# Reordering the grouped-query cross attention of a four-layer model on one Trainium2 core: its first units, the split product, the small turns, and GpSimd's loads

## The chip, the cores and the metric

The program is one launch on one NeuronCore of a Trainium2 chip. The metric is device time in microseconds, the median of several runs. Before the change it is 1155.62 us (three runs, 1152.46 to 1157.61). The engines named below are TensorE (PE for its matmuls, PEld for its weight loads), VectorE (DVE), ScalarE (ACT), GpSimd (POOL) and SyncE (SP), which issues most DMAs. Each runs its own list of instructions in order, and they wait for one another by semaphores.

## The reference, cut to what matters

The model runs twelve blocks on `x` of 2 x 128 tokens with 256 features. The change is in the tenth, `_L3_xattn_ref`, in which the 128 queries of each batch attend to 2048 context rows and to the tokens themselves:

```python
q = (x @ wq).reshape(B, L, 16, 128)
k = (x @ wk).reshape(B, L, 4, 128)
v = (x @ wv).reshape(B, L, 4, 128)
q = rms_norm(q, q_norm_w)
k = rms_norm(k, k_norm_w)
k_ctx = rms_norm((h_ctx_kv @ wk_ctx).reshape(B, T, 4, 128), k_norm_w)
v_ctx = (h_ctx_kv @ wv_ctx).reshape(B, T, 4, 128)
q = q * cos + rotate_half(q) * sin
k = k * cos + rotate_half(k) * sin
k_full = jnp.repeat(jnp.concatenate([k_ctx, k], axis=1), 4, axis=2)
v_full = jnp.repeat(jnp.concatenate([v_ctx, v], axis=1), 4, axis=2)
scores = jnp.einsum('blhd,bmhd->bhlm', q, k_full) * scale + mask
probs = jax.nn.softmax(scores, axis=-1)
out = jnp.einsum('bhlm,bmhd->blhd', probs, v_full)
return out.reshape(B, L, 2048) @ wo
```

All of it is in float32. T is 2048, and `mask` is causal on the tokens' own 128 keys. The last block of the model, a gated feed-forward layer in rounded numbers, has weights that are prepared while this attention runs.

## The kernel before, in words

The class `Wide` holds this block. Its work is cut in two ways. A **unit** `u` (0 to 31) is one head of one batch: 16 chunks of 128 context keys and one chunk of own keys. A **group** `g` (0 to 31) is one quarter (512 rows) of the context of one key head of one batch: its keys are made by `key`, its values by `value`, each with 16 weight loads and 16 matmuls in the trace (one `pe.matmul` of float32 operands shows as two of each). Five groups of keys are made ahead (`FRONT = 5`), so that unit `u` makes group `g = u + 5` beside its own attention.

The **front** (`front_tensor`, and the first lines of `scalar`, `vector` and `gpsimd`) projects the six pieces of batch 0 (keys, four times four query heads, values), rotates them on VectorE (`rope`), scales them on ScalarE (`scale_heads`), turns them on TensorE (`turn_heads`) and copies them back (`copy_turned`). For the keys of groups 0 to 4, ScalarE squares them (`square`), VectorE sums (`sum_squares`), GpSimd takes the inverse root (`scales`), VectorE multiplies (`normalize`), TensorE turns them (`turn_keys`) and ScalarE copies them to their place (`copy_keys`, which raises the semaphore `w_kt`).

The **loop** over the units is in `tensor`. TensorE does, in this order: `scores` of `u` (32 loads and 3 more); `turn_last_output` of `u - 2`; `product` of `u - 1` in three parts (chunks 0 to 8, 9 to 11, 12 to 16, that is 18, 6 and 10 loads), with `turn_largest` of `u` behind the first and `spread_largest` of `u` behind the second; and then `between_tensor`: `turn_keys` of group `g - 1`, `value` of `g`, a wait for `w_kt`, in the first six units one piece of batch 1's projection, in five of them a `turn_heads`, and `key` of `g`.

VectorE's chain in a unit is: largest score of each half (`largest_of`), with `normalize` of group `g - 1` between the two; the larger of both; after `turn_largest` the largest over the partitions; a diagonal matrix of it; after `spread_largest` the copy of the spread row; two additions that shift the scores (`shift`), for which the exponentials of ScalarE and the next unit's `scores` wait. Behind them stand the division of unit `u - 1`, in units 1, 2, 4, 5 and 6 a `rope` of batch 1, and `sum_squares` of group `g`.

From unit 18 on, each unit also prepares one of twelve pieces of the last block's weights: VectorE takes the exponent and a multiple (`weights_exponent`, `weights_multiple`), and GpSimd adds and subtracts (`weights_gpsimd`) and issues the load of the piece after next (`weights_load`), all before its `scales` of the group.

Below, T of a unit is the start of the weight load of its `turn_largest` (L2206 before), Z that of its `spread_largest` (L2211), and S that of its `scores` (L2180).

Of the kernel before, what the change touches and what calls it, by code (L numbers as in the profile page):

```python
# [1892 lines left out]
class Wide:  # L1893
# [180 lines left out]
    def value(self, pe, g, bank):  # L2074
# [7 lines left out]
        for t in range(4):  # L2082
# [3 lines left out]
        last.then_inc(k.s("w_v"), 1)  # L2086
# [55 lines left out]
    def front_tensor(self, pe):  # L2142
# [17 lines left out]
        self.turn_keys(pe, 0, 3)  # L2160
        self.key(pe, 4, 6)
# [29 lines left out]
    def turn_last_output(self, pe, u):  # L2191
# [74 lines left out]
    def tensor(self, pe):  # L2266
        k, s = self.k, self.k.s
        self.front_tensor(pe)
        for u in range(self.UNITS + 1):
            if u < self.UNITS:  # L2270
                self.scores(pe, u)
            if u >= 2:
                self.turn_last_output(pe, u)
            if u >= 1:
                self.product(pe, u - 1, range(0, 9))
# [6 lines left out]
            if u >= 1:  # L2282
                self.product(pe, u - 1, range(12, MC + 1))
# [779 lines left out]
```

## Time and profile before

| what | value |
|---|---|
| median of 3 runs | 1155.62 us (1152.46 to 1157.61) |
| the profiled execution's own time | 1157.82 us |
| its span | 1155.9 us |
| TensorE matmul busy | 1049.1 us (91%) |
| VectorE busy | 700.8 us (61%) |
| ScalarE busy | 503.6 us (44%) |
| GpSimd busy | 232.1 us (20%) |
| front and units of this block | 630.57 to 1086 us of the span |

The durations below come from the profiled execution. Its time is 2.2 us above the median, and its span lies 1.9 us below its time. In a timeline row of the trace the first number is the start in microseconds, the second how long the group of instructions took, then come engine, line, operation and operands, the count, and in brackets the idle time ahead of it with what ended it.

### The profile page before, as it was taken

To read this page: it belongs to the slowest core of one execution; us is meant where nothing else is said; L and a number is where in the kernel's file an instruction comes from. 1 tells how busy PE (TensorE), PEld (TensorE's weight loads), DVE (VectorE), ACT (ScalarE), POOL (GpSimd) and SP (SyncE) were. 2 spreads that over 40 slices of the span, in tenths; PEclk is the share of its full clock that TensorE was granted. 3 is DMA by queue.
4 is the path that set the end of the run, shared out by engine and by line. 5 is a ranking of instruction groups with operands and counts; after the bars stand their busy time and mean duration, and the time that the engine had idled before them with its cause. 6 is when DMAs were issued, how large, how long until landed. Compare 5 with 4: busy or idle time off the path is not lost.

```text
span 1155.9 us, 23193 instructions
## 1 busy us (share of the span) xinstructions
PE 1049.1 (91%) x9488; PEld 847.5 (73%) x9488; DVE 700.8 (61%) x1337; ACT 503.6 (44%) x867; POOL 232.1 (20%) x356
## 2 busy tenths in 40 slices
PE   6899999989999879999987889989999999999885
PEld 3655678865666645677765668889999999999763
DVE  3646242347777358888643766765665566667466
ACT  3042221125666338888754523333233232232374
POOL 4501038402132000000010411210100133332030
PEclk9998999997999979999999989999999999999898
DMA  9711246554663517000141200131111112100000
GB/s 381 292 72 62 87 153 230 182 140 115 181 180 100 170 39 249 3 2 2 38 147 37 92 25 31 37 110 41 53 37 38 55 58 79 57 19 10 1 2 10
DMA packets 39188, 104.57 MB, mean 90 GB/s; under 512 B 4144, under 2 KB 12720, under 8 KB 37424
## 3 DMA queue, kind: packets, MB, share of 16 engines
q1 hardware_dynamic: 35184, 91.55, 24.2%
q0 software_dynamic: 2752, 9.44, 2.4%
q10 hardware_dynamic: 1152, 2.16, 0.5%
q8 instruction: 73, 1.20, 0.4%
q14 instruction: 27, 0.22, 0.1%
HBM read 87.93 MB, written 15.20 MB: 89 GB/s over the span
## 4 chain that ended last, share of the span: by engine, by line
PE 72%; DVE 13%; ACT 4%; issue 4%; POOL 4%; DMA 2%; DVEq 0%; SPq 0%; POOLq 0%; ACTq 0%
PE ps L2225 9%; PE ps L433 7%; PE ps L2180 7%; PE ps L1413 5%; PE ps L1764 5%; PE ps L426 4%; PE ps L2070 4%; PE ps L488 3%; PE ps L1755 3%; PE ps L1561 3%; PE ps L2084 2%; PE ps L1091 2%; PE ps L1099 2%; PE ps L1572 2%; DVE st L1690 2%
## 5 line engine op out<-in xcount | busy, mean ns | idle before, releaser
L2225 PE MATMUL ps<-vv,prob 128*128 128x129 f32 x1024 | 128.7, 274 | 0.0
L2225 PEld LDWEIGHTS ps<-vv,prob 128*128 128x128 f32 x1024 | 122.5, 192 | 0.0
L1690 DVE TENSOR_REDUCE st<-ps 128x1 f32<-128x512 f32 x128 | 83.5, 687 | 27.3 <-PE ps L1561 21.1
L2348 DVE TENSOR_REDUCE probT<-ps 128x128 f32<-128x1024 f32 x64 | 82.6, 1290 | 28.4 <-PE ps L2180 20.4
L2115 ACT ACTIVATE kt<-ps,w 128x512 f32<-128x512 f32 x32 | 22.1, 689 | 141.8 <-PE ps L2092 141.8
L433 PE MATMUL ps<-xT,big 128*128 128x256 f32 x352 | 79.8, 381 | 1.4 <-ACT xT L715 0.7
L2360 DVE TENSOR_TENSOR prob<-ps,probT 128x1024 f32<-128x1024 f32 x64 | 79.6, 1286 | 1.1
L2321 ACT ACTIVATE prob<-prob 128x1024 f32<-128x1024 f32 x64 | 70.8, 1107 | 19.6 <-DVE prob L2360 19.5
L1637 ACT ACTIVATE prob<-ps 128x1024 f32<-128x1024 f32 x64 | 65.8, 1030 | 28.7 <-PE ps L1572 27.0
L152 POOL TENSOR_SCALAR small<-small 128x4 f32<-128x4 f32 (+1 forms) x44 | 12.0, 273 | 325.7 <-DVE small L2122 175.3
L433 PEld LDWEIGHTS ps<-xT,big 128*128 128x128 f32 x352 | 66.4, 190 | 11.8 <-DVE prob L504 1.9
L2070 PE MATMUL ps<-qz,big 128*128 128x128 f32 x512 | 63.0, 277 | 5.0 <-ACT w L1992 2.4
L2070 PEld LDWEIGHTS ps<-qz,big 128*128 128x128 f32 x512 | 59.7, 192 | 9.9 <-ACT w L1992 4.5
L2084 PE MATMUL ps<-qz,big 128*128 128x128 f32 x512 | 62.3, 275 | 0.0
L2180 PE MATMUL ps<-w,kt 128*128 128x128 f32 x512 | 59.9, 275 | 0.8 <-ACT kt L2115 0.8
L2180 PE MATMUL ps<-big,kt 128*128 128x128 f32 x512 | 59.9, 275 | 0.8 <-ACT kt L2115 0.8
L2084 PEld LDWEIGHTS ps<-qz,big 128*128 128x128 f32 x512 | 59.8, 192 | 0.2
L2180 PEld LDWEIGHTS ps<-big,kt 128*128 128x128 f32 x512 | 58.8, 192 | 1.2 <-ACT kt L2115 1.0
L2180 PEld LDWEIGHTS ps<-w,kt 128*128 128x128 f32 x512 | 58.5, 192 | 1.1 <-ACT kt L2115 1.1
L2122 DVE TENSOR_REDUCE small<-probT 128x4 f32<-128x512 f32 x30 | 20.6, 685 | 62.8 <-ACT probT L2105 62.8
L504 DVE TENSOR_TENSOR prob<-prob,ps 128x512 f32<-128x512 f32 x22 | 15.1, 688 | 67.9 <-ACT prob L497 67.8
L2294 ACT COPY w<-ps 128x128 f32<-128x128 f32 x32 | 8.5, 266 | 109.3 <-PE ps L2189 109.3
(456 smaller groups left out, 2216.1 us busy)
## 6 DMA issues: line engine op xcount, KB each, us to landing
big<-ctxT_in SPq DMA_DIRECT2D x36, 512.0 KB, 4.1
big<-blocks_in SPq DMA_DIRECT2D x22, 768.0 KB, 4.4
key_parts<-w POOLq DMA_DIRECT2D x16, 384.0 KB, 5.0
kt<-key_parts SPq DMA_DIRECT2D x32, 192.0 KB, 3.3
vv<-ctx_in SPq DMA_DIRECT2D x2, 2176.0 KB, 27.3
vv<-early_values SPq DMA_DIRECT2D x4, 1088.0 KB, 12.1
kt<-ctxT_in SPq DMA_DIRECT2D x2, 2048.0 KB, 13.2
kt<-key_parts SPq DMA_DIRECT2D x32, 128.0 KB, 3.2
```

Source lines behind the costliest of these rows:

```text
L433: last = pe.matmul(out, w[:, c, lo:lo + P], xT[:, :, c, :], start=(c == 0), stop=(c == DC - 1))
L1413: last = pe.matmul(self.k.ps[g:g + 17, bank, 0:P], self.values(u, ch), pT[:, ch * P:(ch + 1) * P], start=(ch < 4), stop=(ch + 4 >= MC))
L1637: act.activation(self.pT[:, u % 2, h * 1024:(h + 1) * 1024], k.bank(2 + 2 * h, 1024, 2), ACT.Exp).then_inc(s("exp"), 1)
L1690: dve.tensor_reduce(self.mx[:, u % 2, n:n + 1], k.ps[:, n % 2, :], AX.X, ALU.max).then_inc(s("reduced"), 1)
L1764: last = pe.transpose(k.ps[:, bank, ch * P:(ch + 1) * P], self.p[u % 4][:, (4 * n + ch) * P:(4 * n + ch + 1) * P], k.const("ident"))
L2070: last = pe.matmul(k.ps[:, bank, t * P:(t + 1) * P], self.stage[:, g % 2, c, t * P:(t + 1) * P], self.ctx("wk_ctx", DC)[:, c, h * DH:(h + ...
L2084: last = pe.matmul(k.ps[:, bank, t * P:(t + 1) * P], self.stage[:, slot, c, t * P:(t + 1) * P], self.ctx("wv_ctx", DC)[:, c, h * DH:(h + 1 ...
L2180: last = pe.matmul(k.ps[:, ch // 4, ch % 4 * P:ch % 4 * P + P], keys[:, ch * P:(ch + 1) * P], q, start=True, stop=True)
L2225: last = pe.matmul(k.ps[:, 7, 0:DH + 1], self.prob(u)[:, ch * P:ch * P + P], v, start=(ch == 0), stop=(ch == MC))
L2321: act.activation(e, e, ACT.Exp).then_inc(s("c3_exp"), 1)
L2348: dve.tensor_reduce(self.largest[:, h * P:(h + 1) * P], bank.rearrange("p (c t) -> p t c", t=P), AX.X, ALU.max).then_inc(s("c3_max"), 1)
L2360: dve.tensor_tensor(self.prob(u)[:, lo:hi].rearrange("p (c t) -> p c t", t=P), k.bank(0, hi, 5)[:, lo:hi].rearrange("p (c t) -> p c t", t= ...
```

## The change

No arithmetic is added or removed. The instructions of four engines are written in another order.

- In the loop, `turn_last_output` moves behind the first part of `product`, so that it stands beside `turn_largest`; `product` has two parts (chunks 0 to 8, and 9 to 16), and `spread_largest` stands behind the second.
- In `between_tensor` the wait for `w_kt` stands ahead of `value`, in all units. In units 1 and 4 `value` is cut in two halves around the projection; in units 2, 3, 5, 6 and 7 `turn_heads` comes before it; in units 6 and 7 `key` comes before `value`.
- Unit 0 does both small turns behind the projection, and group 4 is normalized in the front.
- In the front, `key` of group 4 takes bank 3 and comes ahead of the turned keys; ScalarE, VectorE and GpSimd follow in a new order.
- GpSimd issues the load of a weight piece behind `scales` of its unit, no longer ahead of it.

```diff
-    def value(self, pe, g, bank):
+    def value(self, pe, g, bank, tiles=range(4)):
...
@@ between_tensor
-        if g not in self.FIRST_VALUES:
-            self.value(pe, g, 5)
+        if u in self.TURN_AT:
+            self.turn_heads(pe, 1, self.TURN_AT[u], 5)
+        elif u in (1, 4):
+            self.value(pe, g, 5, range(0, 2))
         pe.wait_ge(s("w_kt"), g)
         if u < 6:
             self.project(pe, 1, u, 6)
+        if u == 0:
+            self.turn_largest(pe, u)
+            self.spread_largest(pe, u)
+        if u in (6, 7):
+            self.key(pe, g, 6)
         if u in self.TURN_AT:
-            pe.wait_ge(s("w_v_sb"), g + 1)
-            self.turn_heads(pe, 1, self.TURN_AT[u], 5)
+            pe.wait_ge(s("w_q"), 5 + self.TURN_AT[u] + 1)
+        if u >= 1:
+            self.value(pe, g, 5, range(2, 4) if u in (1, 4) else range(4))
         if u < 6:
             pe.wait_ge(s("w_heads"), 6 + u + 1)
-        self.key(pe, g, 6)
+        if u not in (6, 7):
+            self.key(pe, g, 6)
@@ tensor
-            if u >= 2:
-                self.turn_last_output(pe, u)
             if u >= 1:
                 self.product(pe, u - 1, range(0, 9))
-            if u < self.UNITS:
+            if u >= 2:
+                self.turn_last_output(pe, u)
+            if 1 <= u < self.UNITS:
                 self.turn_largest(pe, u)
             if u >= 1:
-                self.product(pe, u - 1, range(9, 12))
-            if u < self.UNITS:
+                self.product(pe, u - 1, range(9, MC + 1))
+            if 1 <= u < self.UNITS:
                 self.spread_largest(pe, u)
-            if u >= 1:
-                self.product(pe, u - 1, range(12, MC + 1))
             self.between_tensor(pe, u)
@@ front_tensor
         self.turn_heads(pe, 0, 2, 2)
-        self.turn_keys(pe, 0, 3)
-        self.key(pe, 4, 6)
+        self.key(pe, 4, 3)
+        self.turn_keys(pe, 0, 6)
         self.turn_keys(pe, 1, 7)
...
@@ scores
+            if u == 0 and ch == 12:
+                pe.wait_ge(s("w_kn"), self.FRONT)
@@ scalar, in the loop
+            if self.TURN_AT.get(u, 0):
+                self.scale_heads(act, 1, self.TURN_AT[u])
             if u >= 2:
                 self.copy_output(act, u - 2, P)
             if g - 1 < self.GROUPS:
                 self.copy_keys(act, g - 1, 6)
...
@@ gpsimd, from unit 18 on
             if u >= self.EIGHT_AT:
                 eight.weights_gpsimd(pool, o, dram, u - self.EIGHT_AT)
             self.scales(pool, o, g)
+            if u >= self.EIGHT_AT:
+                eight.weights_load(pool, dram, u - self.EIGHT_AT + 2)
```

TensorE, a middle unit of the loop from chunk 8 of `product` on, before. L2225 is `product`, L2206 and L2211 the two small turns, L2092 `turn_keys`, L2084 `value`, L2070 `key`, L2180 `scores`.

```order
L2225 MATMUL ps<-vv,prob 128x129 [waits c3_exp]
L2206 MATMUL ps<-const,probT 128x128 [waits c3_max]
L2225 MATMUL ps<-vv,prob 128x129 x3
L2211 MATMUL ps<-probT,const 128x128 [waits c3_max]
L2225 MATMUL ps<-vv,prob 128x129 x4
L2225 MATMUL ps<-probT,prob 128x129
L2092 MATMUL ps<-const,big 128x128 [waits w_kn]
L2092 MATMUL ps<-const,big 128x128 x3
L2084 MATMUL ps<-qz,big 128x128 [waits w_stage0,c3_aT]
L2084 MATMUL ps<-qz,big 128x128 x7
L2070 MATMUL ps<-qz,big 128x128 [waits w_stage0,w_kt]
```

The same unit now (`product` is L2226, the turns L2207 and L2212, `turn_keys` L2093, the turned output L2192).

```order
L2226 MATMUL ps<-vv,prob 128x129 [waits c3_exp]
L2192 MATMUL ps<-const,xn 128x128 [waits c3_finished,w_v_sb]
L2207 MATMUL ps<-const,probT 128x128 [waits c3_max]
L2226 MATMUL ps<-vv,prob 128x129 x7
L2226 MATMUL ps<-probT,prob 128x129
L2212 MATMUL ps<-probT,const 128x128 [waits c3_max]
L2093 MATMUL ps<-const,big 128x128 [waits w_kn]
L2093 MATMUL ps<-const,big 128x128 x3
L2084 MATMUL ps<-qz,big 128x128 [waits w_stage0,w_kt,c3_aT]
L2084 MATMUL ps<-qz,big 128x128 x7
L2070 MATMUL ps<-qz,big 128x128 [waits w_stage0]
```

The spread has moved from between two parts of `product` to its end, and the wait for `w_kt` from the first matmul of `key` to the first of `value`, right behind `turn_keys`.

TensorE, the end of unit 0's scores up to unit 1's, before and now (L426 is the projection).

```order
-L2206 MATMUL ps<-const,probT 128x128 [waits c3_max]
-L2211 MATMUL ps<-probT,const 128x128 [waits c3_max]
-L2092 MATMUL ps<-const,big 128x128 [waits w_kn]
-L2092 MATMUL ps<-const,big 128x128 x3
+L2093 MATMUL ps<-const,big 128x128 [waits w_kn]
+L2093 MATMUL ps<-const,big 128x128 x3
 L426 MATMUL ps<-big,xT 128x512 [waits w_kt]
 L426 MATMUL ps<-big,xT 128x512
+L2207 MATMUL ps<-const,probT 128x128 [waits c3_max]
+L2212 MATMUL ps<-probT,const 128x128 [waits c3_max]
 L2070 MATMUL ps<-qz,big 128x128 [waits w_stage1,w_heads]
```

The two small turns have moved behind the turned keys and the projection, which used to wait for them.

GpSimd in one of the units from 18 on, before: the sum and the difference of a weight piece (L2631, L2632), the load of a piece (L2624) and `scales` (L152, L153).

```order
L2631 TENSOR_TENSOR w<-w,qwrow 128x512 [waits e8_power]
L2632 TENSOR_TENSOR big<-w,qwrow 128x512 [waits pool_order]
L2624 DMA w<-w_in 128x512 [waits e8_w]
L152 TENSOR_SCALAR small<-small 128x4 [waits w_kn,w_ssq]
L153 TENSOR_TENSOR small<-small,const 128x4 [waits pool_order]
```

Now:

```order
L2650 TENSOR_TENSOR w<-w,qwrow 128x512 [waits e8_power]
L2651 TENSOR_TENSOR big<-w,qwrow 128x512 [waits pool_order]
L152 TENSOR_SCALAR small<-small 128x4 [waits w_kn,w_ssq]
L153 TENSOR_TENSOR small<-small,const 128x4 [waits pool_order]
L2643 DMA w<-w_in 128x512 [waits e8_w]
```

The DMA has moved from ahead of `scales` to behind it.

## Rows read from the trace of the kernel before

**Rows 1.** The page's chain that ended last, shares by engine.

```profile
PE 72%; DVE 13%; ACT 4%; issue 4%; POOL 4%; DMA 2%; DVEq 0%; SPq 0%; POOLq 0%; ACTq 0%
```

**Rows 2.** Windows: stretch, length, then busy time (count) by engine, clock, DMA, GB/s.

```profile
800.00:850.00 50.00, 49.87 (x442) 49.05 (x441) 32.10 (x50) 16.59 (x24) 4.81 (x8) 1.00 0.14 43
```

**Rows 3.** Timeline of TensorE's weight loads, unit 9, from T on.

```profile
800.65 0.14 PEld L2206 LDWEIGHTS ps<-const,probT 128*128 128x128 f32 x1
800.76 0.75 PEld L2225 LDWEIGHTS ps<-vv,prob 128*128 128x128 f32 x6
801.73 0.30 PEld L2211 LDWEIGHTS ps<-probT,const 128*128 128x128 f32 x2 [0.23 <-DVE probT L2356]
...
803.51 1.86 PEld L2084 LDWEIGHTS ps<-qz,big 128*128 128x128 f32 x16
```

**Rows 4.** Timeline, VectorE behind the spread of unit 10 (its Z is 814.14).

```profile
814.67 0.29 DVE L2358 COPY probT<-ps 128x128 f32<-128x128 f32 x1 [0.58 <-PE ps L2211]
815.00 2.49 DVE L2360 TENSOR_TENSOR prob<-ps,probT 128x1024 f32<-128x1024 f32 x2
```

**Rows 5.** Timeline, the spread's weight loads of units 1, 8, 18 and 27.

```profile
683.23 0.30 PEld L2211 LDWEIGHTS ps<-probT,const 128*128 128x128 f32 x2 [0.23 <-DVE probT L2356]
...
789.32 0.30 PEld L2211 LDWEIGHTS ps<-probT,const 128*128 128x128 f32 x2 [0.23 <-DVE probT L2356]
...
920.34 0.30 PEld L2211 LDWEIGHTS ps<-probT,const 128*128 128x128 f32 x2 [0.23 <-DVE probT L2356]
...
1037.27 0.30 PEld L2211 LDWEIGHTS ps<-probT,const 128*128 128x128 f32 x2 [0.23 <-DVE probT L2356]
```

**Rows 6.** Timeline, TensorE's loads around `turn_keys` of unit 27.

```profile
1038.61 0.47 PEld L2092 LDWEIGHTS ps<-const,big 128*128 128x128 f32 x4
...
1040.09 3.65 PEld L2180 LDWEIGHTS ps<-big,kt 128*128 128x128 f32 x32 [1.02 <-ACT kt L2115]
```

**Rows 7.** Timeline, units 24 and 25: GpSimd, then VectorE's `normalize`, then TensorE.

```profile
1005.90 0.60 POOL L2624 DMA_DIRECT2D w<-w_in  x1 [0.30 <-POOL big L2632]
...
1006.58 0.19 POOL L152 TENSOR_SCALAR small<-small 128x4 f32<-128x4 f32 x1
...
1007.91 0.69 DVE L2136 TENSOR_TENSOR big<-ps,small 128x512 f32<-128x512 f32 x1 [0.94 <-POOL small L153]
...
1010.25 0.14 PEld L2206 LDWEIGHTS ps<-const,probT 128*128 128x128 f32 x1 [0.54 <-DVE probT L2353]
```

**Rows 8.** Timeline of unit 1, from projection to the scales of its group.

```profile
686.90 1.88 PE L426 MATMUL ps<-big,xT 128*128 128x512 f32 x4
...
689.45 1.86 PEld L2070 LDWEIGHTS ps<-qz,big 128*128 128x128 f32 x16 [1.50 <-ACT qwrow L1992]
...
690.88 0.69 DVE L2017 TENSOR_TENSOR att<-att,small 128x512 f32<-128x512 f32 x1
...
692.17 0.69 DVE L2122 TENSOR_REDUCE small<-probT 128x4 f32<-128x512 f32 x1 [0.59 <-ACT probT L2105]
...
693.23 1.01 POOL L153 TENSOR_TENSOR small<-small,const 128x4 f32<-128x4 f32 x1
```

**Rows 9.** Timeline, end of the front: group 4's square, the first scores.

```profile
655.78 0.60 ACT L2105 ACTIVATE probT<-ps 128x512 f32<-128x512 f32 x1 [0.80 <-PE ps L2070]
...
660.63 3.65 PEld L2180 LDWEIGHTS ps<-w,kt 128*128 128x128 f32 x32 [1.07 <-ACT kt L2115]
```

**Rows 10.** Windows, unit 0.

```profile
667.00:674.00 7.00, 5.43 (x10) 2.42 (x10) 3.25 (x5) 3.10 (x4) 0.00 (x0) 0.51 0.00 0
```

**Rows 11.** Timeline, spread of unit 30 and scores of unit 31.

```profile
1067.40 0.30 PEld L2211 LDWEIGHTS ps<-probT,const 128*128 128x128 f32 x2 [0.22 <-DVE probT L2356]
...
1069.93 3.76 PEld L2180 LDWEIGHTS ps<-big,kt 128*128 128x128 f32 x32
```

**Rows 12.** The page's costliest groups: the exponentials.

```profile
L2321 ACT ACTIVATE prob<-prob 128x1024 f32<-128x1024 f32 x64 | 70.8, 1107 | 19.6 <-DVE prob L2360 19.5
```

**Rows 13.** Timeline, late `turn_heads` of unit 6.

```profile
765.43 0.42 PEld L2036 LDWEIGHTS ps<-const,attT 128*128 128x128 f32 x4 [1.78 <-issue]
```

More of the change, by code:

```diff
@@ L2081, in value @@
         pe.wait_ge(k.s(f"w_stage{slot}"), 16 * loads)
-        for t in range(4):
+        for t in tiles:
             for c in range(DC):
@@ L2085, in value @@
                                  self.ctx("wv_ctx", DC)[:, c, h * DH:(h + 1) * DH], start=(c == 0), stop=(c == 1))
-        last.then_inc(k.s("w_v"), 1)
+        if t == 3:
+            last.then_inc(k.s("w_v"), 1)
     def turn_keys(self, pe, g, bank):
@@ L2271, in tensor @@
                 self.scores(pe, u)
+            if u >= 1:
+                self.product(pe, u - 1, range(0, 9))
             if u >= 2:
                 self.turn_last_output(pe, u)
-            if u >= 1:
-                self.product(pe, u - 1, range(0, 9))
-            if u < self.UNITS:
+            if 1 <= u < self.UNITS:
                 self.turn_largest(pe, u)
             if u >= 1:
-                self.product(pe, u - 1, range(9, 12))
-            if u < self.UNITS:
+                self.product(pe, u - 1, range(9, MC + 1))
+            if 1 <= u < self.UNITS:
                 self.spread_largest(pe, u)
-            if u >= 1:
-                self.product(pe, u - 1, range(12, MC + 1))
             self.between_tensor(pe, u)
@@ L2299, in scalar @@
             self.copy_heads(act, 0, n, bank)
+        self.scale_heads(act, 0, 1)
         self.square(act, 0, 6)
@@ L2302, in scalar @@
         self.copy_turned(act, 0, 0, 0)
-        self.scale_heads(act, 0, 1)
-        self.square(act, 2, 4)
         self.copy_turned(act, 0, 1, 1)
         self.scale_heads(act, 0, 2)
+        self.square(act, 2, 4)
         self.square(act, 3, 5)
         self.copy_turned(act, 0, 2, 2)
-        self.copy_keys(act, 0, 3)
         self.scale_heads(act, 0, 3)
-        self.square(act, 4, 6)
+        self.square(act, 4, 3)
+        self.copy_keys(act, 0, 6)
         self.copy_keys(act, 1, 7)
@@ L2327, in scalar @@
                 self.copy_keys(act, g - 1, 6)
-            if self.TURN_AT.get(u, 0):
-                self.scale_heads(act, 1, self.TURN_AT[u])
+            if u in self.TURN_AT:
+                self.copy_turned(act, 1, self.TURN_AT[u], 5)
+            if u == 0:
+                self.copy_heads(act, 1, u, 6)
             if u < self.UNITS:
                 exp(u, 0)
-            if g < self.GROUPS and g not in self.FIRST_VALUES:
+            if u in (6, 7):
+                self.square(act, g, 6)
+            if 1 <= u < 6:
+                self.copy_heads(act, 1, u, 6)
+            if u >= 8 and g < self.GROUPS:
                 self.copy_value(act, g, 5)
@@ L2335, in scalar @@
                 exp(u, 1)
-            if g < self.GROUPS:
-                if u < 6:
-                    self.copy_heads(act, 1, u, 6)
-                if u in self.TURN_AT:
-                    self.copy_turned(act, 1, self.TURN_AT[u], 5)
+            if 1 <= u < 8:
+                self.copy_value(act, g, 5)
+            if g < self.GROUPS and u not in (6, 7):
                 self.square(act, g, 6)
@@ L2364, in vector @@
         k, s, F = self.k, self.k.s, self.FRONT
-        for n in range(3):
+        for n in range(4):
             self.rope(dve, o, 0, n)
@@ L2368, in vector @@
         self.sum_squares(dve, 1)
-        self.rope(dve, o, 0, 3)
+        self.rope(dve, o, 0, 4)
         for g in range(2):
@@ L2373, in vector @@
         self.sum_squares(dve, 3)
-        self.rope(dve, o, 0, 4)
         for g in range(2, 4):
@@ L2377, in vector @@
         self.sum_squares(dve, 4)
+        self.normalize(dve, 4, self.key_bank(4))
         for u in range(self.UNITS + 1):
@@ L2413, in gpsimd @@
         self.ones(pool, o)
-        for n in (1, 2):
+        for n in (1, 2, 3):
             self.query_scales(pool, o, 0, n)
@@ L2417, in gpsimd @@
             self.scales(pool, o, g)
-            if g % 2:
-                self.query_scales(pool, o, 0, 3 + g // 2)
+            if g == 1:
+                self.query_scales(pool, o, 0, 4)
         for g in range(4, self.GROUPS):
@@ L2619, in weights_load @@
         s = self.k.s
+        if i >= self.PIECES:
+            return
         if i < 2:
```

13 lines of the change are left out of this document (5 added, 8 removed).

## The prediction
> **What bounds the kernel now.** I read the chain of waits first: TensorE has 72% of it [rows 1]. Of windows over the attention, the one over units 9 to 13 shows TensorE busy 49.87 of 50 us at granted clock 1.00 [rows 2]. There the bound is how fast TensorE takes weight loads: 16 of them take 1.86 us, which is 15 spacings of 0.11 and the last one's 0.19 [rows 3]. From here on one load is 0.1116 us. What TensorE waits for must then be looked for in the timeline of weight loads, since the modelled ends of matmuls hide it. In a middle unit that timeline has one gap, ahead of the spread [rows 3]. Unit 8's spread starts at 789.32 and unit 9's at 801.73 [rows 5, 3]: a unit takes 12.41 us, which is 109 loads (12.16), less 0.05 for short ones, and a stall of 0.30. So the stage from unit 8 on is issue with one small stall, units 0 to 7 have larger ones [rows 8, 13], and in units 18 to 27 the spreads stand (1037.27 - 920.34)/9 = 12.99 us apart [rows 5], so something slower than TensorE's own work sets the pace.
>
> **The change, part by part.** I follow T (load of `turn_largest`), Z (load of the spread) and S (first load of scores).
>
> *The spread behind the product.* Six loads after T the spread would have been due at 800.76 + 6 x 0.1116 = 801.43, and it started at 801.73 [rows 3]: 0.30 lost in each unit. With 16 loads between them Z is T + 0.11 + 16 x 0.1116 = T + 1.90, no longer T + 1.08. The diagonal is there by T + 1.08, as it is now, so the stall goes: 12.11 a unit. VectorE's chain behind the spread starts 0.8 later. It has cover where 4 us of turned keys, values and keys stand between Z and the next scores: the first shifted half is done at Z + 0.53 + 0.33 + 1.24 = Z + 2.10 [rows 4]. The turned output moves beside T and is one load in either place.
>
> *The wait for the copied keys ahead of `value`.* This is the price. Before, 16 loads of `value` covered the time in which ScalarE copies the turned keys. Now nothing does. Unit 27 has neither value nor key and so shows this sequence bare: turned keys at 1038.61, the next load at 1040.09, with 1.02 idle put down to the copy [rows 6]. That is 1.48 from the first load of the turned keys, where 0.44 is their own (803.51 is what follows them in unit 9 when nothing waits). Cost: 1.04. On the matmuls' own starts it would be 0.94, which is my lower bound; the upper one is 1.04, which I take since loads set the pace. Units 8 to 17 then take 12.11 + 1.04 = 13.15 instead of 12.41: 10 intervals x 0.74 = +7.4.
>
> *Units 18 to 26.* Their pace is a ring: `normalize`, the second largest, T, spread, shift, exponent and multiple, GpSimd's sum and difference, its load, `scales`, the next `normalize`. Rows 7 show it: the difference ends at 1005.60, the load is issued, `scales` start only at 1006.58, VectorE waits 0.94 for them, and TensorE waits at T. With the load behind `scales` these start at about 1005.66: -0.92. The late spread adds 0.81. The ring becomes 12.99 - 0.92 + 0.81 = 12.88, below TensorE's 13.15, so TensorE sets the pace: 9 x (13.15 - 12.99) = +1.4. GpSimd's gain is eaten by the two others.
>
> *The tail.* Unit 27 was already waiting at its keys; T to S grows by 0.15, as S now waits for the shift at Z + 2.14. Units 28 and 29: T to S is 1.08 + 2.96 before and 1.90 + 2.14 after, nothing. Unit 30 has less output projection to stand behind: 1069.93 - 1067.40 = 2.53 [rows 11] against a least 2.14, so 0.82 - 0.39 = +0.43. Unit 31 passes its 0.82 on. Sum: +1.4, less 0.1 for the turned output that no longer stands ahead of the last product: +1.3.
>
> *Units 1 to 7.* From 683.23 to 789.32 they take 106.09 [rows 5]. A projection costs TensorE 4 x 0.43 = 1.72 [rows 8], a turn of heads 0.44. Before, `key` waited there until the projection had been copied (load at 689.45, idle 1.50, of which 0.94 is lost) [rows 8] or until bank 5 was free (1.78) [rows 13]. The new order puts value behind the projection, which covers both. TensorE's own length becomes 12.11 + 1.72 + 0.07 = 13.9 in units 1 and 4, 12.11 + 1.72 + 0.44 + 0.50 (rest of the wait for the keys) = 14.8 in 2, 3 and 5, and 12.11 + 0.44 + 0.60 = 13.15 in 6 and 7. But in 1, 2, 4, 5 and 6 VectorE has a `rope`: it ended at Z + 8.34 in unit 1 (691.57) [rows 8], and 0.73 earlier without the last multiplication. Behind it come the sum of squares and GpSimd's scales, 694.24 - 692.17 = 2.07 together [rows 8], `normalize` to T 1010.25 - 1007.91 = 2.34 [rows 7], and T to Z 1.80: 14.6 for unit 1 and 13.9 for 4 and 6. The larger of both counts: 14.6 + 14.8 + 14.8 + 13.9 + 14.8 + 13.9 + 13.2 = 100.0. That is -6.1.
>
> *Unit 0.* From S at 660.63 [rows 9] to Z of unit 1 it took 22.60. Now the turned keys and projection run while VectorE looks for the largest: 3.91 for scores, 1.48 for the keys and their copy, 1.72, and 1.04 from T to Z make 8.15. Then the shift to Z + 3.34, an exponential of 1.1 [rows 12] and a square of 0.60 [rows 9], then 2.07 + 2.34 + 1.80 as above: 11.35. Sum 19.5, so -3.1. This supposes the full clock: before, TensorE was granted half of it (1.2 GHz) behind the idle stretches of the scores' turn, 0.51 over 667 to 674 [rows 10], which cost 2.2 of those 22.60. If that stays, the gain is 0.9.
>
> *The front.* ScalarE ends it. From the end of key 4 (655.74) to S took 4.9 [rows 9]. Now the copy of group 0's keys stands in this stretch too, and the last turned heads wait for a scaling right ahead of them: 5.9. Key 4 comes 0.3 earlier, as key 2 does. +0.7, bounds -1 and +3.
>
> The sum is 0.7 - 3.1 - 6.1 + 7.4 + 1.4 + 1.3 = +1.6. The profiled execution has 1157.82 (its span is 1155.9, and 1.9 lie around it), so it would be 1159.4. It lay 2.2 above the median of the runs; on that median, 1155.62, the forecast is 1157.2.
>
> **The rivals.**
> A: the wait at `value` costs far less than 1.04, because something else is late there anyway. Then the 0.30 counts alone and in 18 to 26 the ring of 12.88: -3.0 - 1.0 instead of +8.8 for these nineteen, that is 1144.4. For it speaks only that the wait was harmless before; against it, rows 6.
> B: the first units go at TensorE's own length, since VectorE's steps close up: 1.4 in unit 0 and 0.7 in unit 1, 2.1 together: 1155.1. The idle 0.59 ahead of the sum in unit 1 [rows 8] shows how short VectorE's slack is, which speaks against.
> C: the half clock stays in unit 0, or falls there longer, with front and tail at their upper bounds: 2.2 + 2.3: 1161.7.
> D, the slower side: TensorE's clock falls in units 8 to 27. A stretch such as that of rows 10, 7 us at 0.51, costs up to 3.4 us. TensorE now idles once in every unit. From two stretches on the kernel is slower: 1157.2 + 6.8 = 1164.0. Against it: units 6 and 7 of before idle 1.78 each [rows 13], more than the new 1.0, and the clock stayed at 1.00.
> The Trainium skill, "TensorE: Matmul & The Clock Gate", section "HAM oscillation — how this bites in real kernels", says that gaps inside a loop can throttle TensorE anew in every iteration. By that rule, 19 units with one such stretch each would give 19 x 3.4, some 1220; this trace does not agree for gaps of this size, so it has 1 in 100 within D.
> That the change does not do what it says would be a spread that still waits: it would need a diagonal 0.82 later than now. I give that 2 in 100.
>
> **How the numbers follow.** Forecast 0.62, A 0.08, B 0.12, C 0.08, D 0.08, the spread still waiting 0.02 (with 0.3 x 27 = 8 more, slower). Half a per cent is 5.8 us, about what a measurement of this kernel can tell from no change: below 1149.8 it is faster, above 1161.4 slower. Faster: A whole and 0.05 out of the forecast and B, whose many small steps may add up to one side: 0.13. Slower: D, the last, and a little of C and the forecast: 0.13. Same 0.74. The range: the wait at its lower bound (-1.9), B and the front's -1.7 give 1151.5, C and half of D give 1162; runs of one kernel spread by 5 us, so I take 1149.5 to 1163.
>
> **What would show it.** In the profile of the changed kernel, in units 8 to 17: no gap ahead of the spread, one of about 1.0 ahead of the first `value` load put down to the copy of the keys, and spreads 13.15 apart. In 18 to 26 the same 13.15, no wait of `normalize` that holds TensorE at T. From S(0) to Z(1) 19.5, from Z(1) to Z(8) 100. In units 1, 4 and 6 a gap at T for VectorE. I am wrong if the gap ahead of `value` is under 0.8, if the clock falls below 1.00 between 700 and 1085, or if the front ends over 2 us away from 661.3.

## The result, and the profile after

The forecast was no change, 1157.2 us. The changed kernel takes 1162.26 us (median of 13 runs, 1157.07 to 1167.54); the kernel before, timed beside it, again has a median of 1155.62. The ratio is 1.007 with a 95% interval of 1.005 to 1.0089: slower, by 6.6 us on the medians. The time lies inside the range, near its upper end.

The profiled execution of the changed kernel has 1162.26 us, 4.4 more than that of before. Cut at the same places (F is the first projection load of the front, at 630.57 us before and 627.63 after), the two traces differ as follows. "Forecast" is the term of the prediction.

| stretch | before, us | after, us | difference | forecast |
|---|---|---|---|---|
| start of the span to F | 630.57 | 627.63 | -2.94 | 0 |
| F to S of unit 0 | 30.06 | 31.19 | +1.13 | +0.7 |
| S(0) to Z(1) | 22.60 | 21.58 | -1.02 | -3.1 |
| Z(1) to Z(8) | 106.09 | 100.35 | -5.74 | -6.1 |
| Z(8) to Z(18) | 131.02 | 139.07 | +8.05 | +7.4 |
| Z(18) to Z(27) | 116.93 | 118.95 | +2.02 | +1.4 |
| Z(27) to Z(31) | 39.83 | 40.28 | +0.45 | +1.3 with the next |
| Z(31) to the next block | 12.35 | 14.00 | +1.65 | |
| behind the block | 66.45 | 67.25 | +0.80 | 0 |

The first row is not the change's: before F the two programs are the same. About 1.5 of its 2.94 us arose between 612 and 622 us of before, where the granted clock was 0.66 over 615 to 620; the rest had built up earlier and is not explained. Behind the block the programs are the same again, and the granted clock was 0.89 before and 0.86 after. The seven rows of the block add to +6.54, where the forecast had +1.6. The medians moved by 6.6 too, but that the two agree so closely is in part luck, since both profiled executions lost time to the clock within the block.

The interval from Z(17) to Z(18) also holds the output projection of batch 0. It is 6.9 us longer than the nine ahead of it, before and after, and in every kernel below; "a unit from 8 to 17" means one of those nine.

The chain that ended last, by engine [rows 1]. TensorE's share is up, GpSimd's 4% are gone:

```profile
PE 79%; DVE 11%; issue 4%; ACT 4%; DMA 2%; POOL 0%; DVEq 0%; SPq 0%; ACTq 0%; POOLq 0%
```

The window over the middle units [rows 2]. TensorE is busy 46.70 of 50 us, where it was 49.87, at the same clock:

```profile
800.00:850.00 50.00, 46.70 (x412) 45.82 (x412) 31.17 (x46) 14.95 (x22) 4.80 (x8) 1.00 0.14 43
```

TensorE's weight loads in a middle unit of after, from the turned output (L2192) and T (L2207) to the next spread [rows 3]:

```profile
805.18 0.14 PEld L2192 LDWEIGHTS ps<-const,xn 128*128 128x128 f32 x1
805.29 0.14 PEld L2207 LDWEIGHTS ps<-const,probT 128*128 128x128 f32 x1
805.40 1.64 PEld L2226 LDWEIGHTS ps<-vv,prob 128*128 128x128 f32 x14
...
807.18 0.30 PEld L2212 LDWEIGHTS ps<-probT,const 128*128 128x128 f32 x2
807.41 0.47 PEld L2093 LDWEIGHTS ps<-const,big 128*128 128x128 f32 x4
808.91 1.86 PEld L2084 LDWEIGHTS ps<-qz,big 128*128 128x128 f32 x16 [1.03 <-issue]
...
820.40 0.30 PEld L2212 LDWEIGHTS ps<-probT,const 128*128 128x128 f32 x2
```

The gap ahead of the spread is gone, and one of 1.03 stands ahead of `value`. The trace names "issue" for it, but the load begins as the copy of the turned keys (L2116) ends:

```profile
808.15 0.69 ACT L2116 ACTIVATE kt<-ps,w 128x512 f32<-128x512 f32 x1 [2.29 <-PE ps L2093]
```

From spread to spread it is 820.40 - 807.18 = 13.22 us. The spreads of units 1, 8, 18 and 27 of after [rows 5]:

```profile
680.40 0.30 PEld L2212 LDWEIGHTS ps<-probT,const 128*128 128x128 f32 x2
...
780.75 0.30 PEld L2212 LDWEIGHTS ps<-probT,const 128*128 128x128 f32 x2
...
919.82 0.30 PEld L2212 LDWEIGHTS ps<-probT,const 128*128 128x128 f32 x2
...
1038.77 0.30 PEld L2212 LDWEIGHTS ps<-probT,const 128*128 128x128 f32 x2
```

GpSimd and `normalize` in a unit above 18 [rows 7]. `scales` follow the difference at once, the load is issued behind them, and VectorE no longer waits ahead of `normalize` (L2137):

```profile
1005.16 1.27 POOL L2651 TENSOR_TENSOR big<-w 128x512 bf16<-128x512 f32 x1
1006.51 0.19 POOL L152 TENSOR_SCALAR small<-small 128x4 f32<-128x4 f32 x1
...
1007.79 0.60 POOL L2643 DMA_DIRECT2D w<-w_in  x1
```

```profile
1007.85 0.69 DVE L2137 TENSOR_TENSOR big<-ps,small 128x512 f32<-128x512 f32 x1
```

What the forecast did not have is in the next rows: the end of the front with the scores of unit 0 [rows 9], the end of the block, and windows in both [rows 10], all of after. Thirty-two loads of scores take 3.65 us at full clock and 5.76 here; eight loads of turned keys take 0.91 at full clock and 1.45 here; and the first 18 loads of the last `product` take 3.73 instead of 2.09, behind a wait of 2.97 for the exponential:

```profile
655.80 0.42 PEld L2036 LDWEIGHTS ps<-const,attT 128*128 128x128 f32 x4 [2.47 <-issue]
656.19 1.45 PEld L2093 LDWEIGHTS ps<-const,big 128*128 128x128 f32 x8
658.82 5.76 PEld L2183 LDWEIGHTS ps<-w,kt 128*128 128x128 f32 x32 [1.18 <-ACT kt L2116]
...
1075.04 2.09 PEld L2226 LDWEIGHTS ps<-vv,prob 128*128 128x128 f32 x18
...
1082.98 3.73 PEld L2226 LDWEIGHTS ps<-vv,prob 128*128 128x128 f32 x18 [2.97 <-ACT prob L2329]
```

```profile
656.00:657.00 1.00, 1.00 (x9) 1.00 (x9) 0.00 (x0) 0.50 (x1) 0.05 (x1) 0.73 0.00 0
...
662.00:663.00 1.00, 1.00 (x6) 1.00 (x6) 0.36 (x1) 0.00 (x0) 0.00 (x0) 0.50 0.00 0
663.00:664.00 1.00, 1.00 (x10) 1.00 (x9) 0.86 (x1) 0.00 (x0) 0.00 (x0) 0.86 0.00 0
...
1080.00:1085.00 5.00, 2.40 (x12) 2.03 (x12) 2.83 (x4) 2.22 (x2) 0.00 (x0) 0.81 0.00 0
1085.00:1090.00 5.00, 4.78 (x32) 4.35 (x31) 0.52 (x2) 0.45 (x2) 0.00 (x0) 0.85 0.00 0
```

The half clock began in the turned keys, under 1 us after the wait of 2.47 and ahead of the wait of 1.18, and it ended while the scores were still running: the windows from 657 to 663 us all have 0.50.

### The profile page after: what moved, and what is told of

The parts are those of the page before. It is cut to its first block, busy times and chain, and to the rows that moved or that the text cites. A ratio compares the mean times of both kernels' runs of the same rounds, so it can differ in the third digit from the quotient of the medians.

```text
span 1160.3 us, 23176 instructions
## 1 busy us (share of the span) xinstructions
PE 1045.6 (90%) x9488; PEld 851.0 (73%) x9488; DVE 700.9 (60%) x1337; ACT 507.0 (44%) x867; POOL 232.6 (20%) x356
## 4 chain that ended last, share of the span: by engine, by line
PE 79%; DVE 11%; issue 4%; ACT 4%; DMA 2%; POOL 0%; DVEq 0%; SPq 0%; ACTq 0%; POOLq 0%
PE ps L2226 10%; PE ps L2183 9%; PE ps L433 8%; PE ps L1413 5%; PE ps L1764 5%; PE ps L2084 5%; PE ps L2070 4%; PE ps L426 4%; PE ps L488 3%; PE ps L1755 3%; PE ps L1561 3%; PE ps L1099 2%; PE ps L1091 2%; PE ps L1572 2%; DVE st L1690 2%
## 5 line engine op out<-in xcount | busy, mean ns | idle before, releaser
L2226 PE MATMUL ps<-vv,prob 128*128 128x129 f32 x1024 | 128.2, 278 | 2.6 <-DVE xn L2410 2.6
L2226 PEld LDWEIGHTS ps<-vv,prob 128*128 128x128 f32 x1024 | 121.2, 193 | 3.3 <-ACT prob L2329 3.0
L2084 PE MATMUL ps<-qz,big 128*128 128x128 f32 x512 | 64.0, 278 | 15.7 <-issue 15.7
L152 POOL TENSOR_SCALAR small<-small 128x4 f32<-128x4 f32 (+1 forms) x44 | 13.0, 295 | 324.7 <-DVE small L2123 171.5
L2084 PEld LDWEIGHTS ps<-qz,big 128*128 128x128 f32 x512 | 60.2, 192 | 22.1 <-issue 22.0
L2070 PE MATMUL ps<-qz,big 128*128 128x128 f32 x512 | 62.8, 276 | 3.7 <-DMA big<-ctxT_in 3.0
L2070 PEld LDWEIGHTS ps<-qz,big 128*128 128x128 f32 x512 | 59.7, 192 | 5.3 <-DMA big<-ctxT_in 3.7
L2116 ACT ACTIVATE kt<-ps,w 128x512 f32<-128x512 f32 x32 | 21.9, 688 | 75.0 <-PE ps L2093 74.8
L1561 PE MATMUL ps<-kt,qz 96*128 96x512 bf16 x128 | 47.9, 413 | 7.3 <-DVE st L1690 5.1
```

The costliest lines, as they stand in the source:

```text
L1561: last = pe.matmul(b, self.turned[0:96, u % 2, 1], self.rows[0:96, u % 4, n * 512:(n + 1) * 512], start=True, stop=(n < 3))
L2070: last = pe.matmul(k.ps[:, bank, t * P:(t + 1) * P], self.stage[:, g % 2, c, t * P:(t + 1) * P], self.ctx("wk_ctx", DC)[:, c, h * DH:(h + ...
L2084: last = pe.matmul(k.ps[:, bank, t * P:(t + 1) * P], self.stage[:, slot, c, t * P:(t + 1) * P], self.ctx("wv_ctx", DC)[:, c, h * DH:(h + 1 ...
L2226: last = pe.matmul(k.ps[:, 7, 0:DH + 1], self.prob(u)[:, ch * P:ch * P + P], v, start=(ch == 0), stop=(ch == MC))
```

## The experiments

The theory after the result had four parts. The change is several independent edits, and their sizes add. The wait at `value` costs 1.06 in each unit from 8 on, and costs more than the late spread brings. GpSimd's edit pays by itself but is hidden behind the wait. And the clock took back about 4 us at both ends of the block. The rivals: that the late spread is what costs, that GpSimd's edit does nothing, that the half clock would fall whatever TensorE does in the waits. Nine kernels were run. Their profiled executions, cut as above, in us:

| kernel | F to S(0) | S(0) to Z(1) | Z(1) to Z(8) | Z(8) to Z(18) | Z(18) to Z(27) | Z(27) to Z(31) | to next block |
|---|---|---|---|---|---|---|---|
| value first | 32.39 | 22.11 | 100.33 | 128.46 | 116.16 | 40.28 | 13.98 |
| wait alone | 30.07 | 20.78 | 106.09 | 141.60 | 121.24 | 39.83 | 12.35 |
| loop alone | 30.03 | 22.30 | 104.67 | 128.47 | 124.15 | 40.28 | 12.35 |
| GpSimd alone | 30.12 | 22.98 | 106.08 | 131.01 | 111.68 | 39.83 | 12.35 |
| GpSimd undone | 30.73 | 22.18 | 100.35 | 139.07 | 124.26 | 40.28 | 12.35 |
| filled waits | 30.68 | 19.47 | 100.35 | 139.07 | 118.95 | 40.28 | 12.35 |
| spread at 13 | 30.77 | 21.49 | 99.29 | 128.48 | 110.23 | 38.81 | 12.35 |
| spread at 13, filled | 30.87 | 18.80 | 99.29 | 128.48 | 110.22 | 38.82 | 12.36 |
| first units alone | 30.99 | 21.25 | 101.08 | 131.01 | 116.94 | 39.83 | 12.35 |

("Value first" has 32.39 in its first column because the granted clock was 0.77 and 0.81 over 628 to 636 us of its profiled execution, too.)

**Value first.** The changed kernel, with the values ahead of the wait again from unit 8 on.

```diff
-        pe.wait_ge(s("w_kt"), g)
+        if u < 8:
+            pe.wait_ge(s("w_kt"), g)
...
+        if u >= 8:
+            pe.wait_ge(s("w_kt"), g)
         if u not in (6, 7):
             self.key(pe, g, 6)
```

> The changed kernel with one thing undone: from unit 8 on TensorE makes the values of its group before it waits for the copied keys, as the kernel before does. Theory 1 (the bare wait for the copy is what the change pays in every unit from 8 to 26): the spreads of units 8 to 17 come 12.17 us apart instead of 13.22, those of 18 to 27 at the pace of the ring through VectorE and GpSimd, about 12.9; 10 x 1.05 + 9 x 0.3 = 13 us less, so 1162.3 - 13 = 1149, which is faster than the kernel before. Theory 2 (the loss lies in the front, in unit 0's clock and in the tail, and the gap ahead of the values only replaces another): within 3 us of the changed kernel, 1160 to 1162.

Measured: 1149.53 us (1143.83 to 1153.72), ratio to before 0.9951, interval 0.9931 to 0.9972. A steady unit of it:

```profile
808.88 0.30 PEld L2212 LDWEIGHTS ps<-probT,const 128*128 128x128 f32 x2
809.10 0.47 PEld L2093 LDWEIGHTS ps<-const,big 128*128 128x128 f32 x4
809.54 1.87 PEld L2084 LDWEIGHTS ps<-qz,big 128*128 128x128 f32 x16
```

Nothing stands between the turned keys and the values, and a unit from 8 to 17 takes 12.16. The one wait is worth 139.07 - 128.46 = 10.6 us there and 2.8 in units 18 to 26, where the ring of 12.91 then sets the pace, 13.4 together; the medians lie 12.7 apart. With it gone the change is faster than before.

**Wait alone.** The kernel before, with only that wait put ahead of `value` from unit 8 on.

```diff
+        if u >= 8:
+            pe.wait_ge(s("w_kt"), g)
         if g not in self.FIRST_VALUES:
             self.value(pe, g, 5)
```

> The kernel before with one thing added: from unit 8 on the wait for the copied keys stands ahead of the values. Theory 1: 1.04 in each of ten intervals, and in the nine from unit 18 on TensorE's 12.41 + 1.04 = 13.45 instead of the 12.99 of the ring, +4.1: 1155.6 + 14.5 = 1170. Theory 2: under 5 us more, below 1161.

Measured: 1171.53 us (1169.71 to 1172.33), ratio 1.0143, interval 1.0111 to 1.0175. Both stalls stand in one unit:

```profile
801.62 0.30 PEld L2211 LDWEIGHTS ps<-probT,const 128*128 128x128 f32 x2 [0.23 <-DVE probT L2358]
...
804.45 1.86 PEld L2084 LDWEIGHTS ps<-qz,big 128*128 128x128 f32 x16 [1.03 <-issue]
```

The unit takes 13.47, which is 12.41 + 1.06: the wait does not depend on where the spread is. In units 18 to 26 it is 13.47 as well, where 12.99 was the pace; both stretches together lose 14.9, and the median lies 15.5 above that of before timed beside it. This kernel's unit 0 ran at full clock in its profiled execution, though the instructions there are those of before [rows 10]:

```profile
667.00:674.00 7.00, 3.96 (x17) 2.23 (x18) 3.48 (x6) 3.38 (x4) 0.00 (x0) 1.00 0.00 0
```

S(0) to Z(1) is then 20.78 instead of 22.60. So unit 0 of before costs 1.8 more where the clock falls, and the clock need not fall there in every execution.

**Loop alone.** The kernel before, with the loop in the new order.

```diff
         for u in range(self.UNITS + 1):
...
-            if u >= 2:
-                self.turn_last_output(pe, u)
             if u >= 1:
                 self.product(pe, u - 1, range(0, 9))
+            if u >= 2:
+                self.turn_last_output(pe, u)
             if u < self.UNITS:
                 self.turn_largest(pe, u)
             if u >= 1:
-                self.product(pe, u - 1, range(9, 12))
+                self.product(pe, u - 1, range(9, MC + 1))
             if u < self.UNITS:
                 self.spread_largest(pe, u)
-            if u >= 1:
-                self.product(pe, u - 1, range(12, MC + 1))
```

> The kernel before with the new order of the loop alone: product in two parts, turned output beside the turned largest, spread behind the product, in all units; first units, front, GpSimd and the wait ahead of the keys as before. Theory 1: the stall of 0.30 ahead of the spread goes but the turned output costs 0.06 more, so -0.24 in 17 units (-4), while the ring of units 18 to 26 gets 0.81 longer, 13.80 (+7.3), and the tail 0.5: 1155.6 + 3.7 = 1159.3, with spreads 12.17 apart in units 8 to 17 and 13.80 in 18 to 27. Rival (no ring there, TensorE alone sets the pace): -0.24 in 26 units, 1149.5.

Measured: 1161.16 us (1158.87 to 1162.59), ratio 1.0051, interval 1.0032 to 1.0069. Units 8 to 17 take 12.16, 0.25 less each; units 18 to 26 take 13.8, and T waits there for VectorE:

```profile
1007.82 0.14 PEld L2206 LDWEIGHTS ps<-const,probT 128*128 128x128 f32 x1 [1.65 <-DVE probT L2351]
1009.66 0.30 PEld L2211 LDWEIGHTS ps<-probT,const 128*128 128x128 f32 x2
```

That is the ring of the prediction: 12.99 and 0.81 more for the later spread. The loop's new order (late spread and moved turned output) gains 2.6 in units 8 to 17 and loses 7.2 in units 18 to 26. From Z(1) to Z(31) the profile has +3.7, as expected; the medians have +5.1, and the 1.4 between them is not explained.

**GpSimd alone.** The kernel before, with the load behind `scales`.

```diff
     def weights_gpsimd(...):
-        if i + 2 < self.PIECES:
-            self.weights_load(pool, dram, i + 2)
...
             self.scales(pool, o, g)
+            if u >= self.EIGHT_AT:
+                eight.weights_load(pool, dram, u - self.EIGHT_AT + 2)
```

> The kernel before with GpSimd's order alone: the load of a weight piece behind the scales of its unit. Theory 1: the ring of units 18 to 26 gets 0.92 shorter, 12.07, and TensorE's 12.41 sets the pace: 9 x 0.58 = 5.2 us less, 1150.4, with no wait of TensorE ahead of the turned largest. Rival (GpSimd is off the path): no change, 1155.6.

Measured: 1150.75 us (1145.13 to 1152.82), ratio 0.9956, interval 0.9936 to 0.9976. Units 18 to 26 take 12.40 instead of 12.99: the ring has become shorter than TensorE's own 12.41. Its GpSimd in one of these units:

```profile
1007.81 0.19 POOL L152 TENSOR_SCALAR small<-small 128x4 f32<-128x4 f32 x1
1008.09 1.02 POOL L153 TENSOR_TENSOR small<-small,const 128x4 f32<-128x4 f32 x1
1009.08 0.60 POOL L2629 DMA_DIRECT2D w<-w_in  x1
```

**GpSimd undone.** The changed kernel with the load ahead of `scales` again (the lines of "GpSimd alone" backwards).

> The changed kernel with GpSimd's order undone (the load of a weight piece ahead of the scales again). Theory 1: TensorE's 13.22 a unit no longer covers the ring, which is 13.75 with the late spread (as in the kernel with the loop alone): 9 x 0.53 = 4.8 us more than the changed kernel, 1167. Rival (the bare wait for the keys hides all of GpSimd's order): no change, 1162.

Measured: 1165.75 us (1162.14 to 1168.52), ratio 1.0087, interval 1.0057 to 1.0117. Units 18 to 26 are at 13.8 again, and T waits again. The wait at `value` is still in each unit and costs nothing in these, since the ring is longer than TensorE's 13.22:

```profile
1001.15 0.14 PEld L2207 LDWEIGHTS ps<-const,probT 128*128 128x128 f32 x1 [0.63 <-DVE probT L2367]
1002.99 0.30 PEld L2212 LDWEIGHTS ps<-probT,const 128*128 128x128 f32 x2
```

The profiles have 5.3 us more than the changed kernel in these nine units. The medians have 3.5 more, with ratio intervals that overlap, so the size is read from the profiles alone.

**Filled waits.** The changed kernel with transposes of the identity, whose results nobody reads, in TensorE's waits of the front (11, 7, 5 and 20 of them) and ahead of the last `product` (20).

```diff
+    def fill(self, pe, bank, n):
+        for i in range(n):
+            pe.transpose(k.ps[:, bank, i % 4 * P:i % 4 * P + P], k.const("ident"), k.const("ident"))
...
+        self.fill(pe, 4, 11)
         self.key(pe, 2, 4)
+        self.fill(pe, 5, 7)
         self.key(pe, 3, 5)
...
+        self.fill(pe, 3, 5)
         self.key(pe, 4, 3)
...
         pe.wait_ge(s("w_q"), 2)
+        self.fill(pe, 1, 20)
         self.turn_heads(pe, 0, 4, 1)
...
+        if u == self.UNITS - 1:
+            pe.wait_ge(s("c3_aT"), self.UNITS - 2)
+            for i in range(20):
+                pe.transpose(k.ps[:, 5, 2 * P + i % 2 * P:3 * P + i % 2 * P], k.const("ident"), k.const("ident"))
```

> The changed kernel with idle time of TensorE filled: 11, 7, 5 and 20 turns of the identity into free banks in four waits of the front, and 20 ahead of the last product; they feed nothing. Theory 1 (two stretches at half clock, in unit 0 and in the last product, come of the idle time ahead of them and are paid in most runs): granted clock 1.00 in both, scores of unit 0 in 3.65 instead of 5.76 us and the last product's first part in 2.1 instead of 3.73: 3.7 us less, 1158.5. Rival (they fall by chance or for another reason): no change, 1162, with 0.5 somewhere near as before.

Measured: 1158.66 us (1153.61 to 1161.87), ratio 1.0032, interval 1.0009 to 1.0056. The median is 3.6 below that of the changed kernel; the intervals of the two ratios overlap a little. The granted clock of the whole execution has a median of 0.976 over its twelve runs and 0.970 over the thirteen of the changed kernel, so the fall is not the profiled execution's alone. Its loads and windows at both ends (L2178 and L2258 are the transposes, L2192 the scores):

```profile
652.56 2.21 PEld L2178 LDWEIGHTS ps<-const 128*128 128x128 f32 x20
655.00 0.42 PEld L2036 LDWEIGHTS ps<-const,attT 128*128 128x128 f32 x4 [0.23 <-ACT attT L2026]
655.39 0.90 PEld L2093 LDWEIGHTS ps<-const,big 128*128 128x128 f32 x8
657.50 3.65 PEld L2192 LDWEIGHTS ps<-w,kt 128*128 128x128 f32 x32 [1.21 <-ACT kt L2116]
...
1076.61 2.32 PEld L2258 LDWEIGHTS ps<-const 128*128 128x128 f32 x20
1079.55 2.08 PEld L2235 LDWEIGHTS ps<-vv,prob 128*128 128x128 f32 x18 [0.62 <-issue]
```

```profile
655.00:660.00 5.00, 4.03 (x35) 3.79 (x35) 1.10 (x2) 1.75 (x3) 0.31 (x1) 1.00 0.01 3
...
1075.00:1080.00 5.00, 4.59 (x39) 4.23 (x38) 3.21 (x5) 2.06 (x2) 0.00 (x0) 1.00 0.00 0
```

The clock stays at 2.4 GHz, the scores take 3.65, and S(0) to Z(1) is 19.47. The stretches from Z(1) to Z(31) are those of the changed kernel. For the front this is shown: the clock fell there in all five profiled executions that have this front without filling (the changed kernel, "value first", "GpSimd undone", "spread at 13" and "first units alone"), and in neither of the two with it. Which of the four filled waits matters was not tested. For the last `product` nothing is shown, since "loop alone" and "GpSimd undone" have the same wait (2.96 and 2.97) and took 2.08 for the 18 loads without any filling. The fall there comes in some executions and not in others.

**Spread at 13, and the same filled.** Value first, with the spread behind chunk 13 in place of 16: ten loads behind T instead of sixteen. T + 0.11 + 10 x 0.1116 is 1.23, still behind the 1.08 at which the diagonal is there, and 0.67 earlier for VectorE's ring. The second kernel has the transposes too.

```diff
             if u >= 1:
-                self.product(pe, u - 1, range(9, MC + 1))
+                self.product(pe, u - 1, range(9, 14))
             if 1 <= u < self.UNITS:
                 self.spread_largest(pe, u)
+            if u >= 1:
+                self.product(pe, u - 1, range(14, MC + 1))
```

> The changed kernel with the values ahead of the wait from unit 8 on, and with the spread behind chunk 13 of the product, 10 loads after the turned largest, where the diagonal is just ready. Theory 1: units 8 to 17 stay at 12.16, the ring of 18 to 26 falls from 12.91 to about 12.25 (-6.0), VectorE's chain in units 0, 1 and 6 is 0.67 shorter each (-2.0), tail -1.6: 1149.5 - 9.6 = 1140. Rival (the place of the spread is worth only its stall of 0.3): no gain over 1149.5.

> The kernel with the values first and the spread behind chunk 13, with the idle time filled as in the run with filled waits. Theory 1: 3.7 us less than without the fill, 1136. Rival: as without the fill, 1140.

Measured: 1138.97 us (1136.19 to 1139.87), ratio 0.9852, interval 0.982 to 0.9883; and filled 1135.71 us (1135.22 to 1140.05), ratio 0.9835, interval 0.9803 to 0.9868. A middle unit of the first has no idle time at all:

```profile
806.10 0.14 PEld L2207 LDWEIGHTS ps<-const,probT 128*128 128x128 f32 x1
806.21 1.20 PEld L2226 LDWEIGHTS ps<-vv,prob 128*128 128x128 f32 x10
807.33 0.30 PEld L2212 LDWEIGHTS ps<-probT,const 128*128 128x128 f32 x2
```

The windows of the second, over unit 0 and over the middle units:

```profile
660.00:665.00 5.00, 4.22 (x35) 3.73 (x34) 2.87 (x3) 0.69 (x1) 0.00 (x0) 1.00 0.00 0
800.00:850.00 50.00, 50.00 (x451) 49.95 (x450) 32.34 (x50) 16.84 (x25) 4.81 (x8) 1.00 0.13 43
```

TensorE is busy 50.00 of 50 us, units 8 to 17 take 12.16 (109 loads), units 18 to 26 take 12.24. The rival of the first is out: the ring went from 12.91 to 12.25. The second is the best version, 19.3 us below the kernel before timed beside it. The transposes' own share (1138.97 to 1135.71) is not shown by the medians, since it is read from six runs each whose ranges overlap; in the profiles it is the 2.7 us of unit 0.

**First units alone.** The kernel before with the new front and the new `between_tensor` of units 0 to 7 only: "value first" with the loop of before and GpSimd's old order.

> The kernel before with the new front and the new between-work of units 0 to 7 alone; from unit 8 the values go ahead of the wait for the copied keys, product has its three parts with the spread behind chunk 11, the turned output stands ahead of it, and GpSimd issues each load ahead of its scales. Theory (the first units' gain is their own and does not hang on the loop's order): front +1.1, unit 0 -1 where the clock falls and -3 where not, units 1 to 7 99.6 to 101.0 us instead of 106.09 (those that VectorE sets lose 0.5 each, the others gain a stall of 0.3), units 8 to 17 12.41 and 18 to 26 12.99 as before, the tail as before: sum -5 to -7, about 1150. Rival (the first units only gain because the spread stands behind the product): units 1 to 7 at 104 or more, 1154 or more.

Measured: 1151.70 us (1146.62 to 1155.21), ratio 0.9976, interval 0.9958 to 0.9993. Units 1 to 7 take 101.08:

```profile
682.20 0.30 PEld L2212 LDWEIGHTS ps<-probT,const 128*128 128x128 f32 x2 [0.23 <-DVE probT L2375]
...
783.28 0.30 PEld L2212 LDWEIGHTS ps<-probT,const 128*128 128x128 f32 x2 [0.23 <-DVE probT L2375]
```

The profile has about the expected gain, 5.0 us in units 1 to 7 (101.08, where at most 101.0 was expected) and 5.4 in the block, and the rival's 104 for these units is out. On the medians the gain is about 2 to 3 us, with an interval from 0.8 to 4.8; what lies between is not explained. Part of it may be the clock. It fell in unit 0 here too (6.23 us for the 32 loads of scores), as in all profiled executions of the new front without filling, while with the old front it fell in three of four. The granted clock of the whole execution has a median of 0.972 here and 0.975 in the seventeen runs of before; 0.003 of 1150 us is an estimate of up to 3.4 us more lost, which would close the gap. That was not tested by itself.

## Why the prediction was wrong, point by point

The block was forecast at +1.6 and came out at +6.5. By the prediction's own steps:

*The spread behind the product*: right. The gap is gone, and "loop alone" gains 0.25 per unit.

*The turned output "is one load in either place"*: off by 0.05. Ahead of `product` it put that off by 0.05 to 0.06 (811.93 to 811.99 in "wait alone"); beside T it puts T off by a whole 0.11 (805.18 to 805.29). A unit of "value first" took 12.16, for 12.11. With the wait's 1.06 for 1.04 the forecast of 13.15 became 13.22. Over nineteen units the two are 1.3 us, which is what units 8 to 17 (+8.05 for +7.4) and 18 to 26 (+2.02 for +1.4) are off by.

*The wait for the copied keys, 1.04*: right to 0.02, and from one row of unit 27 [rows 6]. "Wait alone" measured 1.06.

*The ring of units 18 to 26*: right in each part. With GpSimd's load moved alone the ring drops out of sight, with the spread moved alone it grows by 0.8, and only the new wait made TensorE the slower one.

*Units 1 to 7, -6.1*: -5.74. The single units came at 14.54, 14.92, 14.91, 14.08, 14.91, 13.79 and 13.20 for 14.6, 14.8, 14.8, 13.9, 14.8, 13.9 and 13.2. VectorE is what the next T waits for at the end of unit 1 (T of unit 2) and of unit 6 (T of unit 7), as forecast. In unit 4, where a gap at T was forecast too, there is none, and TensorE's own work makes the 14.08:

```profile
693.10 0.14 PEld L2207 LDWEIGHTS ps<-const,probT 128*128 128x128 f32 x1 [0.48 <-DVE probT L2367]
...
765.71 0.14 PEld L2207 LDWEIGHTS ps<-const,probT 128*128 128x128 f32 x1 [0.61 <-DVE probT L2367]
```

*The tail, +1.3*: the 0.82 by which the spread comes later was counted twice: the stretches up to Z(27) end at the spread and so hold it already, and it was added again as what "unit 31 passes on". Without it 0.5 was to be forecast, and +0.45 came.

*Unit 0, -3.1*: this is the step that failed. The working was right: with the waits filled the stretch is 19.47, for a forecast of 19.5. But the term "supposes the full clock", and it booked as a gain of the change the 2.2 us that before had lost to the half clock (1.8 by "wait alone": 22.60 against 20.78). No edit of the change filled TensorE's idle time. It moved it: before, the idle stretches were in unit 0 itself, and now the longest, of 2.47, is at the end of the front, so the half clock begins there and falls on most of the scores, 32 loads in one piece. It costs 2.1 there and 0.5 on the turned keys ahead of them. "If that stays, the gain is 0.9" was the right branch: the gain was 1.02. It should have been the forecast, and rival C with its 0.08 the likeliest case for this stretch. At full clock on both sides the new order is worth 20.78 - 19.47 = 1.3.

*The last product*: not in the prediction, which gave nothing for the clock there. The wait ahead of it grew from 1.85 to 2.97, as ten loads of `product` that stood behind the last spread now stand ahead of it. The clock fell behind that wait and cost 1.65 us, in the changed kernel and in "value first", and not in "loop alone" and "GpSimd undone", which have the same wait (2.96 and 2.97) there. Why it falls in some executions stays open.

Added up: unit 0 2.1, the last product 1.65, the turned output and the wait 1.3, the front 0.4 (with the 0.5 of the turned keys in it), units 1 to 7 0.4, the tail -0.85: 5.0, for the 4.9 that were missing. Of the rivals, A is out (the wait costs all of its 1.04), B too (T of unit 1 waits 1.36 for VectorE and T of unit 2 waits 0.48), the spread no longer waits, and D in its form is out: with 1.03 of idle time in each of nineteen units the clock stayed at 1.00. The Trainium skill, "TensorE: Matmul & The Clock Gate", section "HAM oscillation — how this bites in real kernels", shows a loop that is throttled anew in every pass behind DMA waits of some 3 to 5 us. The waits of 1.03 here are shorter, so the trace does not contradict the section, as the prediction had it; no run here has a loop with waits as long as those.

C came nearest, at 1161.7, and its number is luck: its 2.3 from front and tail at their upper bounds did not come (they were off by +0.4 and -0.85), and other terms filled their place. Of the signs of being wrong that the prediction named, two came true: the clock fell below 1.00 ahead of 1085 (0.56 over 1083 to 1084), and the front ended at 658.82, 2.5 from 661.3. The second is mostly the earlier F; from F on the front was 0.4 longer than forecast.

## What to carry to other kernels

When one change holds edits for several stages, price each by the stage's own bound, and then ask of each pair whether one hides the other: here GpSimd's reorder was worth 5 us alone, the split of the loop 2.6 in the units where the ring does not bind, and a wait that was set for all units alike cost 13.4 in the nineteen where nothing covers it. An operation moved behind others should go just as far as its operand needs (here 10 loads, not 16), since a chain on another engine starts from it. And a stretch at half clock in the profile of before is not a gain to be booked until something is named that keeps TensorE busy there.

## What the runs showed of the hardware that was not expected

A wait of 1.03 in every 13.22 us left TensorE's granted clock at 1.00 for nineteen units. In the front of the changed kernel it went from 2.4 to 1.2 GHz under 1 us after a wait of 2.47 and was back some 7 us later, before the scores had ended; with the 2.47 and three shorter waits ahead of it filled with transposes it stayed at 2.4, though the wait of 1.21 right ahead of the scores was still there. The same instructions need not get the same clock in two executions: unit 0 of the old order had 0.51 in one kernel [rows 10] and 1.00 in "wait alone", and the first 18 loads of the last `product` took 3.73 us in the changed kernel and 2.08 in "GpSimd undone", behind the same 2.97 of waiting.
